# Causal cross attention without a mask on the turned scores: GpSimd zeroes the masked probabilities

## The reference, cut to what matters

```python
Q = _rope((query @ w_q + b_q).reshape(b, s, 16, 8).transpose(0, 2, 1, 3), token_positions)
K = _rope((key @ w_k + b_k).reshape(b, s, 16, 8).transpose(0, 2, 1, 3), token_positions)
V = (value @ w_v + b_v).reshape(b, s, 16, 8).transpose(0, 2, 1, 3)
scores = jnp.einsum('bhqd,bhkd->bhqk', Q, K) / jnp.sqrt(jnp.float32(8))
causal = jnp.tril(jnp.ones((s, s), dtype=bool))
scores = jnp.where(causal, scores, -jnp.inf)
attn = jax.nn.softmax(scores, axis=-1)
out = jnp.einsum('bhqk,bhkd->bhqd', attn, V)
x = _layernorm(x + out.transpose(0, 2, 1, 3).reshape(b, s, 128) @ w_o + b_o)
```

## Time and profile before

| What | Value |
|---|---|
| Time of three runs | 1739.76, 1743.04, 1743.62 us (median 1743.04) |
| Span of the profiled execution | 1740.7 us, mean granted TensorE clock 0.939 |
| Busy over the span | PE 1516.1 us (87%), PEld 1088.4 us, DVE 1273.2 us (73%), ACT 1069.6 us (61%), POOL 691.6 us (40%) |
| L2x, first to last masked step | about 989 to 1157 us from the span's start |

### The profile page before, as it was taken

One profiled execution on the slowest core, in us unless ns is written; L12 is line 12 of the kernel. 1 busy time (PEld: TensorE's weight loads), 2 busy tenths in 40 slices (PEclk: granted clock), 3 DMA queues, 4 the chain that ended last, 5 costly groups with the idle time before them and its releaser, 6 DMA issues.

```text
span 1740.7 us, 34480 instructions
## 1 busy us (share of the span) xinstructions
PE 1516.1 (87%) x12731; PEld 1088.4 (63%) x12741; DVE 1273.2 (73%) x2817; ACT 1069.6 (61%) x2219; POOL 691.6 (40%) x801
## 2 busy tenths in 40 slices
PE   6588868799998898889989999998989998989875
PEld 5344436578777555667768766665548994655542
DVE  2688863697775798479999667758873448858988
ACT  4499942367665577399999155546763443157765
POOL 2455635578887022356767313320000101511223
PEclk9799979899999999989898989999998999999985
DMA  3200121200000000010000100000000000000000
GB/s 133 111 13 14 37 93 37 61 10 2 1 1 1 2 2 2 4 37 1 1 1 1 58 2 2 2 13 1 2 2 1 1 1 11 1 19 2 2 2 25
DMA packets 14791, 30.94 MB, mean 18 GB/s; under 512 B 1537, under 2 KB 10145, under 8 KB 13857
## 3 DMA queue, kind: packets, MB, share of 16 engines
q1 hardware_dynamic: 13602, 26.63, 4.4%
q0 software_dynamic: 1024, 2.10, 0.4%
HBM read 22.42 MB, written 6.29 MB: 16 GB/s over the span
## 4 chain that ended last, share of the span: by engine, by line
PE 44%; DVE 15%; ACT 14%; issue 12%; POOL 12%; DMA 1%; SPq 0%; POOLq 0%; DVEq 0%; ACTq 0%
PE PS L1412 5%; PE PS L1472 4%; ACT big L2261 4%; POOL big L837 4%; DVE negmax L2802 3%; PE PS L1744 3%; PE PS L1733 3%; POOL big L825 3%; ACT big L2239 2%; PE PS L1494 2%; POOL big L833 2%; PE PS L1417 2%; PE PS L1911 2%; PE PS L1895 2%; DVE V L3383 2%
## 5 line engine op out<-in xcount | busy, mean ns | idle before, releaser
L2239 ACT ACTIVATE big<-PS 128x1024 f32<-128x1024 f32 (+1 forms) x256 | 249.0, 974 | 163.4 <-PE PS L1423 162.7
L2802 DVE TENSOR_REDUCE negmax<-PS 128x4 f32<-128x1024 f32 x192 | 235.0, 1224 | 54.3 <-PE PS L1412 52.2
L1412 PE MATMUL PS<-KS,QS 32*128 32x256 f32 (+1 forms) x1152 | 133.2, 316 | 36.1 <-DVE negmax L2802 25.9
L1412 PEld LDWEIGHTS PS<-KS,QS 32*128 32x128 f32 x1152 | 86.7, 187 | 109.7 <-DVE negmax L2802 71.5
L711 POOL TENSOR_TENSOR rstd<-veps,mhalf 128x2 f32<-128x2 f32 x72 | 51.3, 712 | 242.2 <-DVE veps L2676 232.7
L1423 PE MATMUL PS<-QS,KS 32*128 32x256 f32 (+1 forms) x1152 | 133.7, 319 | 1.4 <-ACT big L2239 1.4
L1472 PE MATMUL PS<-big,V 128*32 128x256 f32 (+1 forms) x2048 | 133.0, 378 | 0.4 <-ACT big L2239 0.4
L737 POOL TENSOR_TENSOR res<-resb,XB 128x256 f32<-128x256 f32 x24 | 17.4, 727 | 258.5 <-ACT resb L2325 258.5
L779 POOL TENSOR_SCALAR KT<-QT 128x1024 f32<-128x1024 f32 x64 | 66.6, 1040 | 66.6 <-DVE QT L2821 62.7
L2821 DVE SCALAR_TENSOR_TENSOR QT<-PS,wint 128x1024 f32<-128x1024 f32 x64 | 77.3, 1220 | 17.9 <-PE PS L1365 17.2
L1423 PEld LDWEIGHTS PS<-QS,KS 32*128 32x128 f32 x1152 | 84.8, 188 | 5.8 <-issue 4.0
(11 more groups left out here) (479 smaller groups left out, 4323.8 us busy)
## 6 DMA issues: line engine op xcount, KB each, us to landing
W<-in_wpack SPq DMA_DIRECT2D x1, 4180.0 KB, 13.9
W<-in_wpack SPq DMA_DIRECT2D x1, 2560.0 KB, 9.0
W<-in_wpack SPq DMA_DIRECT2D x1, 2449.5 KB, 8.0
y_rows<-one_more SPq DMA_DIRECT2D x1, 2048.0 KB, 9.0
masks<-in_mask SPq DMA_DIRECT2D x8, 256.0 KB, 2.9
x_rows<-x_tok SPq DMA_DIRECT2D x16, 128.0 KB, 2.1
W<-in_wpack SPq DMA_DIRECT2D x1, 1538.0 KB, 5.9
x_tok<-in_x SPq DMA_DIRECT2D x1, 1024.0 KB, 4.8
```

The lines of the kernel that those rows point to most:

```text
L1412: mm = nc.tensor.matmul(PS[:, MAXB[half], o], QS[r, bm % 2, tm, j * P:(j + 1) * P], KS[r, bm % 2, tm, k], start=not a.causal, stop=last)
L2239: nc.scalar.activation(PX[:, T % 2, 2 * p:2 * p + 2, 0:cols], PS[:, exp_banks(g)[0]:exp_banks(g)[0] + 2, 0:cols], ACT.Exp, scale=a.scale). ...
L2802: ins = nc.vector.tensor_reduce(negmax[:, h:h + 2, :].rearrange("p h j -> p (h j)"), banks.rearrange("p h (j k) -> p (h j) k", j=2), AX.X, ...
```

## The change

The turned scores get no mask: the two `causalT` matmuls of a step go, and the `turned` matmuls start their accumulation themselves. Two turned matmuls of 128 columns each, which share their keys, become one of 256. The exponentials of masked places are then whatever the scores give, and GpSimd writes 0 over them in `PX`: `zero_masked(g)` issues two `affine_select` (one for each head, 128 x 2 x 128 floats). `values(T)` waits for a new semaphore, `t_cut`, in place of `t_probs`. GpSimd's program for this stage is now a loop over the same steps as the others: in a step it does `turns`, `low_part`, `zero_masked(g - 5)`, `skip`, `residual`, then the inverse root and `normalise`, each if it is due. In stage L0x the semaphore `t_low` is only renamed to `t_cut`.

```diff
-                def turns(b):
-                    for o, k in enumerate((1, 0)):
-                        pool.wait_ge(sem("t_read"), at("t_read", 2 * b + o + 1))
...
+                def turns(b, o):
+                    k = 1 - o
+                    pool.wait_ge(sem("t_read"), at("t_read", 2 * b + o + 1))
...
+                def zero_masked(g):
+                    T, p = g // 2, g % 2
+                    pool.wait_ge(sem("t_probs"), at("t_probs", g + 1))
+                    for half in range(2):
+                        diagonal = PX[:, T % 2, 2 * p + half, :].rearrange("p (a c) -> p a c", a=2)[:, :, 0:P]
+                        ins = nc.gpsimd.affine_select(out=diagonal, in_=diagonal, compare_op=ALU.is_ge, fill=0.0,
+                                                      base=0, pattern=[[0, 2], [1, P]], channel_multiplier=-1)
+                    ins.then_inc(sem("t_cut"), 1)
+                if a.causal:
+                    for g in range(TURN_X_AT, last_step(a) + 2):
+                        for o in range(2):
+                            if (b := due(g, a.turn_unit_at[o] + 2)) is not None:
+                                turns(b, o)
+                        if (b := due(g, a.project_at)) is not None:
+                            low_part(b)
+                        if 0 <= g - a.lag < PAIRS * B:
+                            zero_masked(g - a.lag)
+                        if (b := due(g, 10)) is not None:
+                            skip(b)
+                        if (b := due(g, a.y_at + 1)) is not None:
+                            residual(b)
+                        if (b := due(g, a.y_at + 2)) is not None:
+                            inverse_root(n, b)
+                            normalise(b)
+                    return
                 for i in range(-2, B + 2):
-                    if a.rope and 0 <= i + 1 < B:
-                        low_part(i + 1)
-                    if a.rope and i + 2 < B:
-                        turns(i + 2)
...
                     if a.causal:
                         for half in range(2):
                             if m:
                                 mask(MAXB[half], causal[:, 0, 0:P])
-                        for half in range(2):
-                            if e:
-                                mask(exp_banks(ge)[half], causalT[:, :])
                         if m:
                             maximum(slice(0, P), 0, slice(0, P), False)
                         if e:
-                            turned(0, slice(0, P), slice(0, P), False)
+                            turned(0, slice(0, S), slice(0, S))
...
                         if e:
-                            turned(1, slice(2 * P, 3 * P), slice(P, S), False)
-                            turned(0, slice(P, S), slice(P, S)).then_inc(sem("t_turned"), 1)
+                            turned(1, slice(2 * P, 3 * P), slice(P, S)).then_inc(sem("t_turned"), 1)
...
-                    pe.wait_ge(sem("t_probs"), at("t_probs", (4 if a.clip else 2) * (T + 1)))
+                    if a.causal:
+                        pe.wait_ge(sem("t_cut"), at("t_cut", 2 * (T + 1)))
+                    else:
+                        pe.wait_ge(sem("t_probs"), at("t_probs", (4 if a.clip else 2) * (T + 1)))
```

More of the change, by code:

```diff
@@ L242, in counts @@
         if a.clip:
-            each.update(t_clipped=8, t_low=8, t_probs=16, t_cap=1, t_cap_psum=1, t_capT=1)
+            each.update(t_clipped=8, t_cut=8, t_probs=16, t_cap=1, t_cap_psum=1, t_capT=1)
         else:
@@ L249, in counts @@
             each.update(t_proj_psum=1)
+        if a.causal:
+            each.update(t_cut=8)
         if a.tail:
@@ L744, in normalise @@
                     ins.then_inc(x_done, 1)
-                def turns(b):
-                    for o, k in enumerate((1, 0)):
-                        pool.wait_ge(sem("t_read"), at("t_read", 2 * b + o + 1))
-                        if b >= 2:
-                            pool.wait_ge(sem("t_lo"), at("t_lo", 2 * (b - 1)))
-                        nc.gpsimd.tensor_tensor(KT[:, 2 * (b % 2) + k, :], QT[:, 2 * k, :], QT[:, 2 * k + 1, :], ALU.add)\
-                          .then_inc(sem("t_rope"), 1)
+                def turns(b, o):
+                    k = 1 - o
+                    pool.wait_ge(sem("t_read"), at("t_read", 2 * b + o + 1))
+                    if b >= 2:
+                        pool.wait_ge(sem("t_lo"), at("t_lo", 2 * (b - 1)))
+                    nc.gpsimd.tensor_tensor(KT[:, 2 * (b % 2) + k, :], QT[:, 2 * k, :], QT[:, 2 * k + 1, :], ALU.add)\
+                      .then_inc(sem("t_rope"), 1)
                 def low_part(b):
@@ L779, in low_scores @@
                     nc.gpsimd.tensor_scalar(clipped(KT, g), clipped(QT, g), LOW_TOP / a.scale, -2 * BIG, ALU.min, ALU.max)\
-                      .then_inc(sem("t_low"), 1)
+                      .then_inc(sem("t_cut"), 1)
                 def clear_v():
@@ L1418, in mask, with turned @@
                                          what.unsqueeze(1).broadcast_to([P, 2, P]), start=True, stop=False)
-                    def turned(kb, o, q, last=True):
+                    def turned(kb, o, q):
                         for half in range(2):
@@ L1423, in turned @@
                             mm = nc.tensor.matmul(PS[:, exp_banks(ge)[half], o], KS[r, be % 2, te, kb * P:(kb + 1) * P],
-                                                  QS[r, be % 2, te, q], start=not a.causal, stop=last)
+                                                  QS[r, be % 2, te, q], start=True, stop=True)
                         return mm
@@ L2259, in clip_exponentials @@
                     else:
-                        act.wait_ge(sem("t_low"), at("t_low", g + 1))
+                        act.wait_ge(sem("t_cut"), at("t_cut", g + 1))
                     nc.scalar.activation((PX, PX2)[k][:, T % 2, 2 * p:2 * p + 2, :], clipped((QT, KT)[k], g), ACT.Exp,
@@ L2819, in clip @@
                         dve.wait_ge(sem("t_probs"), at("t_probs", 2 * (g - 2) + 1))
-                        dve.wait_ge(sem("t_low"), at("t_low", g - 1))
+                        dve.wait_ge(sem("t_cut"), at("t_cut", g - 1))
                     nc.vector.scalar_tensor_tensor(clipped(QT, g), PS[:, pair_banks(g):pair_banks(g) + 2, :], -100.0 / a.scale,
```

## The result

The changed kernel took 1765.36 us (median of 4 runs, 1752.72 to 1770.37), the kernel before 1743.13 beside it. The ratio is 1.0102, with a 95% interval of 1.0071 to 1.0133: about 1% slower, and outside the forecast range of 1735 to 1752 us. In a second set of 12 runs the same kernel had a ratio of 1.0074 (1.0042 to 1.0107). The profiled execution took 1760.93, its span is 1759.2.

The account below looks back on a forecast made before the run. TensorE's list set the pace, or nearly, in a ring with VectorE's maxima. Terms -13.3 + 5.5 + 3.2 + 3.5 = -1.1 us gave 1741.9 against the median 1743.04, range 1735 to 1752.

Parts of the forecast that it names:

- the sum, -1.1 us: Whole kernel: masks -13.3, late residual +5.5, VectorE held up +3.2 and clock +3.5; gains and losses nearly cancel, chance 0.38.
- The masks that go: TensorE in L2x: 0.23 us saved a step without the causalT pair, counted 58 times, -13.3 us.
- the 0.5 to 1.5 forecast: Early in the stage, a batch without a clock fall some 0.5 to 1.5 us shorter than 19.77.
- The selections: GpSimd: 0.40 us each, 0.80 a pair, 6.4 us more per batch; no bound, values' wait costed at nothing.
- The residual is late: Step 8b+21, batches 0 to 5: residual behind selections delays statistics, maxima and masks, 0.92 us each, +5.5 (+2.6 to +8.2).
- VectorE held up: VectorE's small instructions and statistics slowed beside GpSimd's selections: +2.0 and +1.2, together +3.2 us, bounds 0 and +6.
- Its part at `low_part`: `low_part` one step later, behind `turns`, meets L2789 and L2790: 0.4 us each, 5 times, +2.0 us.
- The clock: TensorE's granted clock falls in longer waits behind late residuals: two falls at 1.75 us, +3.5, bounds 0 and +12.
- the short fall of the earlier trace: TensorE's clock in the profile before: a window of 4 us at 0.65, costing 1.4 us.
- one fall at 10 us: TensorE's clock: a fall of up to 10 us at half speed costs up to 5 us.
- The rival of falls at the late residuals: Clock falls at most of six late residuals; five falls at 2.5 us give +7.9, so 1751 us; chance 0.25.

Follow-up runs that it names:

- the two halves: Kernel before with causalT matmuls gone and nothing else: 0.9948; changed kernel with those matmuls back as filler that computes nothing: 1.0045.
- the doubled ones: Changed kernel with the residual ahead of the selections, plus a second selection of the same shape beside each of the 128: ratio 1.0033, 1752.06 us.
- The half with filler: Changed kernel with the two causalT matmuls back in each step of L2x, overwritten so that they compute nothing; selections stay: ratio 1.0045, 1751.15 us.
- the wait filled: Changed kernel, residual still late, with ten unused matmuls in TensorE's wait behind step 8b+22 of batches 0 to 5: ratio 0.9959, 1738.74 us.
- the masks alone: Kernel before with causalT matmuls gone and turned scores in two matmuls instead of three, no selections; output not the reference's: ratio 0.9948, 1738.57 us.
- the residual first: Changed kernel with the residual ahead of the selections of its step on GpSimd, all else kept: ratio 0.9945, 1735.78 us.
- its second profile: Profiled execution of the changed kernel run again without edit, the slowest of its twelve: stage 198.6 us; the set's ratio was 1.0074.

## Why the prediction was wrong

The masks and the late residual were forecast well step by step. What was missed is what they do to the clock together. That the sum, -1.1 us, is also what the two halves measured separately give (-1.2) is partly luck: without its clock term the sum is -4.6, the two halves give -14.6 + 6.3 = -8.3 in the traces of the stage, and only more low clock elsewhere (+17 and +23 over all runs) brings the ratios to -1.2.

- **The masks that go, -13.3**: right in the stage. Alone they shorten the stage by 14.6 us, of which 0.4 x 3 = 1.2 is a little less low clock; the whole kernel gains 9.1. An undisturbed batch of the changed kernel takes 19.03 us in the chain of waits (L1349 at 1064.81 and 1083.84) against 19.77, 0.74 less, inside the 0.5 to 1.5 forecast.
- **The selections, 0.80 a pair**: right, 0.78. Nobody waited for them, and GpSimd was no bound; the doubled ones show that its limit is close.
- **The residual is late, +5.5**: the path was right step by step. In the late batch the statistics came at +3.03 (forecast +3.12), the masks at +5.04 (forecast +5.26), TensorE idle for 1.70 (forecast 2.0). In an early batch TensorE was idle 0.79 (forecast 1.1).
- **VectorE held up, +3.2**: too dear. The two losses together were forecast as +8.7. The half with filler gave a stage 6.3 us longer (7.8 us in the ratio), and with the residual late, all selections there and the wait filled the stage is 5.5 longer than with the masks alone (173.8 - 168.3); the late residual's +5.5 leaves little for VectorE. Its part at `low_part` didn't appear: of the two small instructions the first took 271 ns in the mean before and 192 in the changed kernel (L2789, now L2812), the second 268 and 326 (L2790, now L2813), no more together (1000 to 1180 us, 31 to 33 of each). The hold-up itself is there. In the trace an L2813 that starts beside a selection ends 0.02 to 0.03 us after it, in 0.26 us instead of 0.17, and the last instruction of the statistics (L2699) takes 0.24 instead of 0.17 in five batches, 0.07 more where 0.2 was forecast. With the residual first, all 128 selections cost 2.2 us in the stage against none (170.5 - 168.3), and 7 us more of low clock would explain that alone.
- **The clock, two falls at 1.75, +3.5, bounds 0 to +12**: this is the step that failed, in number, in size and in its upper bound. The text took the short fall of the earlier trace rows as the likely one and one fall at 10 us as the dearest. There were six stretches, 3.4 to 20.5 us long, five of them new. The low clock in the 190 us grew by 42 us over the kernel before, at 0.40 each 17 us, where the term had 3.5. From the filled wait to the changed kernel the stage grows by 18.1 us, and to its second profile by 24.8 (198.6 - 173.8), where the bound was 12. The rival of falls at the late residuals (1751) came nearest to the mechanism; its price, 2.5 each, was too small, and only two or three of the falls stand right behind a late residual's wait. The wait was part of the cause (fill it or take it away, and the falls go) but not a sufficient one: the half with filler has three waits of 1.6 us and one fall of 6.8 behind the last. The text had noted that the missing masks were activity too, and gave it no price.
- **What came behind the stage** had no term. L3a lost 7.5 us in both traces of the changed kernel. It lost as much with the masks alone, which has no new fall in L2x, so the falls there aren't needed for it. This part is shown for single executions only.

The Trainium skill, "TensorE: Matmul & The Clock Gate", Part 1, states that the throttled clock is the default and that activity releases it. The runs agree: matmuls without a use gave 18 us back in the stage where they stood in the wait, and none where they stood four steps off.

What stays open: how the missing masks and the idle piece share the cause. Each alone leaves the clock of the stage up, no run varied the masks' amount, and no rule that says when a single fall begins comes out of the traces: one wait of 1.72 us had no fall behind it, and two falls had no wait before them.

## What to carry to other kernels

Taking work off TensorE and making it wait once a batch are two changes whose prices couldn't be added here. A way to allow for it: read the longest idle piece of TensorE per period before and after, and if it grows while work goes, count every period as a possible fall, at 0.4 us for each us at the low level (the price in this stage), not at the length of the shortest fall in the trace. On an in-order engine put the instruction that somebody waits for ahead of the new work in the same step; here that one move turned +0.7 to +1.0% into -0.5% in ten of twelve runs. A handful of matmuls that compute nothing, once in the wait and once elsewhere, is a good test of whether a loss is the clock's; read the clock over all runs, not in one trace.

## What the runs showed that was not expected

- In the traces of the stage neither half of the change moved the clock by much (8 and 15 us low of 190, before 11); both together gave 53 and 72. Over all runs and the whole kernel the halves cost 23 and 17 us of low clock, and both together 61.
- Ten matmuls of 256 columns in the wait, six times (three waits were 1.7 us, three 0.8 or less), removed 45 us of low clock. The same ten elsewhere removed none.
- The same kernel spreads by 1.6% from run to run (before, 1732.67 to 1760.02 in 35 runs), and in these 35 the time grows by 0.34 us for each us of low clock (from the granted clock and span of each run). The order of two kernels that are half a per cent apart is in the mean, not in one trace.
- With a pad of thirteen matmuls in front of L3a, the one profiled execution of the kernel before had a fall of 20.5 us, for 7.6 us, some 65 us later. Over all its runs the low clock was 3 us more.
